# Preparing an attention stage inside the feed-forward before it, and another order of TensorE's work in each quad

## The reference

```
q = layernorm(x);  k = v = context                       # 16 blocks of 128 rows, causal in a block
scores = q @ k.T * 16**-0.5, masked;  p = exp(scores - max) / sum
x = x + tanh(g_xattn[1]) * (p @ v)
```

## Time and profile before

| | us |
|---|---|
| median of 3 runs | 1004.36 (1002.21 to 1005.16) |
| the profiled execution | 1005.2 |
| its span | 1003.1 |
| TensorE busy (PE) | 927.2, 92% of the span |
| VectorE busy (DVE) | 605.9, 60% |
| ScalarE busy (ACT) | 522.6, 52% |
| GpSimd busy (POOL) | 188.5, 19% |

### The profile page before, as it was taken

How to read it: one execution, slowest core, us unless ns; L and a number is a source line. 1 busy time by engine, 2 the same in 40 slices (tenths; PEclk the granted TensorE clock), 3 DMA queues, 4 the chain that set the end, 5 groups by cost and what they waited for, 6 DMA issues and landing times. The chain is left out here.

```text
span 1003.1 us, 14109 instructions
## 1 busy us (share of the span) xinstructions
PE 927.2 (92%) x4800; PEld 744.1 (74%) x4816; DVE 605.9 (60%) x1411; ACT 522.6 (52%) x938; POOL 188.5 (19%) x162
## 2 busy tenths in 40 slices
PE   6799889999999999778888886999999999999998
PEld 6799768877888888645555564787778888888886
DVE  6677654465645655367777754565865556555554
ACT  3222044433543333357677543666666676666665
POOL 5899200000000000166666400000000000000000
PEclk8899999999999999999999988999999999999999
DMA  9100110323211321225444213334444434544443
GB/s 309 35 1 1 64 64 17 110 86 110 69 49 48 106 80 47 95 81 157 150 143 131 94 64 100 127 126 126 140 144 128 140 106 137 147 143 141 145 128 116
DMA packets 58535, 105.43 MB, mean 105 GB/s; under 512 B 7360, under 2 KB 13888, under 8 KB 58080
## 3 DMA queue, kind: packets, MB, share of 16 engines
q1 hardware_dynamic: 57744, 104.39, 32.6%
q10 hardware_dynamic: 720, 0.14, 0.1%
HBM read 102.08 MB, written 2.42 MB: 104 GB/s over the span
## 5 line engine op out<-in xcount | busy, mean ns | idle before, releaser
L740 DVE TENSOR_TENSOR ylof<-yf,yhif 128x512 fp32r<-128x512 f32 x200 | 138.2, 691 | 176.2 <-ACT yhif L653 175.8
L884 PE MATMUL bank<-xhf,whif 128*128 128x512 f32 x528 | 212.2, 402 | 1.5 <-ACT rf L628 1.5
L884 PE MATMUL bank<-xlf,whif 128*128 128x512 f32 x528 | 208.7, 395 | 0.0
L884 PE MATMUL bank<-xhf,wlof 128*128 128x512 f32 x528 | 208.6, 395 | 0.0
L913 PE MATMUL bank<-yhif,whif 128*128 128x512 f32 x400 | 160.1, 400 | 13.0 <-DVE ylof L740 12.9
L653 ACT ACTIVATE yhif<-yf 128x512 fp32r<-128x512 f32 x200 | 125.5, 628 | 89.1 <-DVE yf L753 82.4
L913 PE MATMUL bank<-yhif,wlof 128*128 128x512 f32 x400 | 157.9, 395 | 0.0
L913 PE MATMUL bank<-ylof,whif 128*128 128x512 f32 x400 | 157.0, 393 | 0.0
L630 ACT ACTIVATE rf<-bank 128x512 f32<-128x512 f32 x136 | 81.6, 600 | 125.0 <-PE bank L884 124.2
L884 PEld LDWEIGHTS bank<-xhf,wlof 128*128 128x128 f32 x528 | 99.8, 189 | 24.0
L884 PEld LDWEIGHTS bank<-xhf,whif 128*128 128x128 f32 x528 | 99.4, 188 | 24.5 <-ACT rf L628 1.9
(11 more groups left out here) (129 smaller groups left out, 1197.2 us busy)
## 6 DMA issues: line engine op xcount, KB each, us to landing
Gf<-gates SPq DMA_DIRECT2D x160, 256.0 KB, 3.7
wrawf<-in_wu SPq DMA_DIRECT2D x68, 256.0 KB, 2.6
k_blocks_sb<-in_k_blk SPq DMA_DIRECT2D x64, 256.0 KB, 4.1
wrawf<-in_wu SPq DMA_DIRECT2D x32, 384.0 KB, 3.1
v_slot<-in_v_rows SPq DMA_DIRECT2D x16, 256.0 KB, 2.6
ctx_windows<-in_ctx_win SPq DMA_DIRECT2D x3, 1024.0 KB, 10.8
toeplitz<-in_kpad SPq DMA_DIRECT2D x4, 512.0 KB, 9.3
X<-in_x SPq DMA_DIRECT2D x4, 512.0 KB, 9.3
```

The lines of the kernel that those rows point to most:

```text
L740: dve.tensor_tensor(ylo[:, K % S, :], y[:, K % S, :], yhi[:, K % S, :].bitcast(F32), ALU.subtract).then_inc(s_yl, 1)
L884: last = pe.matmul(o, w_[:, Nu % S, wc], x_[:, c, xs], start=(m == 0), stop=(m == 5))
```

## The change

1. The attention's tiles and semaphores for keys, values and queries are set up ahead of f0, and its steps become functions that f0 can call: load_keys, key_hi, key_lo, query_normed, query_hi, query_lo, query_turned and query_copy (before: keys, k_hi, k_lo, normed, x_hi, x_lo, queries, q_copy).
2. In f0, SP issues six key loads, the mask, the bf16 identity and two value loads at step K = 48 (NK - 16). In the last twelve steps ScalarE and TensorE do three blocks' query_normed and query_hi, two blocks' query_turned and query_copy and four quads' key_hi; GpSimd does the low halves.
3. The last four pieces of f0's output are no longer turned and added in f0. Its tile (os_) outlives the stage, and the attention does this in its first quads: ffn_turned on TensorE and ffn_added on VectorE, interleaved with quads 0 to 3. variances("c", 1) and what follows from it move behind them.
4. The attention's keep_clock and first queries go. ScalarE's first instruction is an Exp on a small tile.
5. TensorE's order in iteration n becomes turned(n), scores(n+2), values(n). query_turned(b+2) comes in a block's last quad, a block earlier than before, and so do query_normed, query_hi and query_lo (b+3) on ScalarE and GpSimd. out_copy(b-1) and query_copy(b+1) are done in a block's first quad, the one ahead of and the other behind probs.

```diff
                     for j in range(BPB):
                         residual(NB - BPB + j)
 
+
+        pn = ExitStack()
...
+        def load_keys(sp, n):
+            if n >= KLR:
+                sp.wait_ge(s_k2, n - KLR + 1)
+            sp.dma_start(KM[:, n % KLR, :], k_blk[n]).then_inc(s_kl[n % KLR], 16)
+
+        def load_values(sp, b):
+            if b >= 2:
+                sp.wait_ge(s_pv, 4 * (b - 2) + 4)
+            sp.dma_start(V[:, b % 2].rearrange("p h d -> p (h d)"), v_rows[b]).then_inc(s_vl[b % 2], 16)
...
+        def key_hi(act, n):
+            act.wait_ge(s_kl[n % KLR], LOADED + 16 * (n // KLR + 1))
+            if n >= KR:
+                act.wait_ge(s_s, n - KR + 1)
+            act.activation(K1[:, n % KR, :], KM[:, n % KLR, :], ACT.Copy).then_inc(s_k1, 1)
...
+        def key_lo(pool, n):
+            pool.wait_ge(s_k1, n + 1)
+            pool.tensor_tensor(K2[:, n % KR, :], KM[:, n % KLR, :], K1[:, n % KR, :].bitcast(F32),
+                               ALU.subtract).then_inc(s_k2, 1)
...
+        def query_normed(act, b):
+            act.wait_ge(s_sh, b // (2 * BPB) + 1)
+            if b >= 2:
+                act.wait_ge(s_lo, b - 1)
+            act.activation(xc[:, b % 2, :], X[:, b, :], ACT.Identity, bias=nshift[:, b:b + 1],
+                           scale=rstd[:, b:b + 1]).then_inc(s_n, 1)
...
+        def query_lo(pool, b):
+            pool.wait_ge(s_hi, b + 1)
+            pool.tensor_tensor(xs[:, b % 2, :, 1, :], xc[:, b % 2, :].rearrange("p (q f) -> p q f", q=4),
+                               xs[:, b % 2, :, 0, :].bitcast(F32), ALU.subtract).then_inc(s_lo, 1)
+
+        def query_turned(pe, b):
+            pe.wait_ge(s_lo, b + 1)
+            if b > 0:
+                pe.wait_ge(s_qt, b)
+            for t in range(4):
+                last = pe.transpose(x_bank[:, t * P:(t + 1) * P],
+                                    xs[:, b % 2, t].rearrange("p s f -> p (s f)").bitcast(F32), ident[:])
+            last.then_inc(s_xt, 1)
...
+        def query_copy(act, b):
+            act.wait_ge(s_xt, b + 1)
+            if b >= 2:
+                act.wait_ge(s_s, 4 * (b - 1))
+            act.activation(Q1[:, b % 2].rearrange("p t q -> p (t q)"), x_bank, ACT.Copy, scale=SCALE1).then_inc(s_qt, 1)
...
+        def attention_loads(sp):
+            for n in range(KLR):
+                load_keys(sp, n)
+            sp.dma_start(causal[:], causal_c).then_inc(s_cc, 16)
+            sp.dma_start(identb[:], identb_c).then_inc(s_cc, 16)
+            load_values(sp, 0)
+            load_values(sp, 1)
+
+        def attention_ahead_act(act, left):
+
+            if left in (12, 11, 4):
+                query_normed(act, {12: 0, 11: 1, 4: 2}[left])
+            if left in (11, 10, 3):
+                query_hi(act, {11: 0, 10: 1, 3: 2}[left])
+            if left in (9, 8, 7, 6):
+                key_hi(act, 9 - left)
+            if left in (6, 3):
+                query_copy(act, {6: 0, 3: 1}[left])
+
+        def attention_ahead_pe(pe, left):
+
+            if left in (8, 5):
+                query_turned(pe, {8: 0, 5: 1}[left])
+
+        def attention_ahead_pool(pool):
+            query_lo(pool, 0)
+            query_lo(pool, 1)
+            for n in range(KR):
+                key_lo(pool, n)
+            query_lo(pool, 2)
...
+                def out_turned(pe, p, s, i, dst):
+                    pe.wait_ge(s_os, 2 * p + s + 1)
+                    for j in (2 * i, 2 * i + 1):
+                        for c in range(2):
+                            last = pe.transpose(dst[:, (j % 2) * D + c * P:(j % 2) * D + (c + 1) * P],
+                                                os_[:, s, c, j * P:(j + 1) * P], ident[:])
+                    last.then_inc(s_ot, 1)
+
+                def out_added(dve, p, s, i, src):
+                    n = 4 * p + 2 * s + i
+                    dve.wait_ge(s_ot, n + 1)
+                    b0 = n * 2
+                    xv = X[:, b0:b0 + 2, :].rearrange("p b d -> p (b d)")
+                    dve.tensor_tensor(xv, src, xv, ALU.add).then_inc(s_xa, 1)
+                    if not final:
+                        dve.wait_ge(s_xa, n + 1)
+                        for b in (b0, b0 + 1):
+                            dve.bn_stats(stats[:, b, :], X[:, b, :]).then_inc(s_xs, 1)
+
...
@@ -598,6 +733,8 @@
                                 if GATES_STORE[m] == K:
                                     store_gates(m)
                             gate_rows(K)
+                            if not final and K == NK - 16:
+                                attention_loads(sp)
...
                         if not final:
                             deviations(pool, "c", 0)
                             shifts(pool, "c", 0)
+                            attention_ahead_pool(pool)
...
+                            if not final:
+                                attention_ahead_act(act, NK - K)
                         if not gated:
...
@@ -867,9 +999,10 @@
                                 negated(dve, "c", 0)
                         if not gated:
                             y_lo(NK - 1)
-                        for s in range(2):
-                            for i in range(2):
-                                residual(1, s, i, bk(2 * s + i))
+                        if final:
+                            for s in range(2):
+                                for i in range(2):
+                                    residual(1, s, i, bk(2 * s + i))
...
-                        pe.wait_ge(s_xa, 4)
-                        for s in range(2):
-                            for i in range(2):
-                                out_t(1, s, i, bk(2 * s + i))
+                            if not final:
+                                attention_ahead_pe(pe, NK - K)
+                        if final:
+                            pe.wait_ge(s_xa, 4)
+                            for s in range(2):
+                                for i in range(2):
+                                    out_t(1, s, i, bk(2 * s + i))
+
+            return out_turned, out_added, s_xa, s_xs
...
 
             def turn_bank(n):
                 return bk(4 + n % 2)
@@ -1172,70 +1280,27 @@
             with nc.Block() as block:
                 @block.sync
...
-                    vals(1)
                     for n in range(KLR, NQ):
-                        keys(n)
-                        if n % 4 == 0 and n // 4 + 1 < NB and n // 4 >= 2:
-                            vals(n // 4)
-                    vals(NB - 1)
+                        load_keys(sp, n)
+                        if n % 4 == 0 and n // 4 >= 2:
+                            load_values(sp, n // 4)
 
                 @block.gpsimd
...
                     for n in range(NQ):
                         b, t = n // 4, n % 4
                         if n + KR < NQ:
-                            k_lo(n + KR)
-                        if t == 3 and b + 2 < NB:
-                            x_lo(b + 2)
+                            key_lo(pool, n + KR)
+                        if t == 3 and b + 3 < NB:
+                            query_lo(pool, b + 3)
+                        if n == 4:
+                            deviations(pool, "c", 1)
+                            shifts(pool, "c", 1)
                         if n == 4 * 10:
                             deviations(pool, "f1", 0)
 
...
-                    keep_clock(pe, bk(0), 20)
-                    queries(0)
                     pe.wait_ge(s_cc, 32)
                     scores(0)
                     scores(1)
+                    ffn_turned(pe, 1, 0, 0, o_bank)
+                    ffn_turned(pe, 1, 0, 1, row_bank)
                     for n in range(NQ):
                         b, t = n // 4, n % 4
+                        turned(n)
                         if n + 2 < NQ:
                             scores(n + 2)
-                        turned(n)
-                        if n > 0:
-                            values(n - 1)
-                        if t == 0 and b + 1 < NB:
-                            queries(b + 1)
+                        if n == 0:
+                            pe.wait_ge(s_ffn_x, 5)
+                        values(n)
+                        if n in (1, 2):
+                            pe.wait_ge(s_ffn_x, 5 + n)
+                            ffn_turned(pe, 1, 1, n - 1, row_bank)
+                        if t == 3 and b + 2 < NB:
+                            query_turned(pe, b + 2)
+                        if n == 6:
+                            pe.wait_ge(s_ffn_x, 8)
                         if t == 2 and b > 0:
                             out_rows(b - 1)
-                    values(NQ - 1)
                     out_rows(NB - 1)
...
-                    normed(0)
-                    x_hi(0)
-                    k_hi(0)
-                    normed(1)
-                    k_hi(1)
-                    q_copy(0)
-                    x_hi(1)
-                    k_hi(2)
-                    k_hi(3)
```

(87 more changed lines are left out.)

91 lines of the change are left out of this document (9 added, 82 removed).

## The result

The changed kernel takes 974.59 us (median of 4 runs, 973.37 to 975.51) against 1004.02 (4 runs) for the kernel before on the same chip: a ratio of 0.9708 with a 95% interval of [0.9689, 0.9726]. The forecast was 975. The profiled execution took 974.85, with a span of 972.7 in place of 1003.1.

A forecast was written before the change was run, and what follows sets the result against it. The attention's stride was taken as bound by the order in which engines wait for each other, none full. Start 14.9 plus stride 15.4 less tail 0.8 made 29.5 off 1005.2, 975.7, stated as 975; range 967 to 986.

The forecast's parts named there:

- f0's end: In f0's last steps, two added query_turned cost 0.9 us; the other work put there is hidden.
- Start: Where f0 ends and the attention begins: turned(6) comes at 431.1 instead of 446.01, 14.9 us less.
- the ten short instructions: On VectorE in the attention's start, variances and negated between shifted(4) and maxima(5): an estimated 0.8 us.
- Stride: Attention's 14 blocks, turned(6) to turned(62): 7.7 us a block, 108.2 in all against 123.6, 15.4 less.
- a new wait: In each attention quad, values wait 0.18 us for probs of the same quad: 1.35 from turned against TensorE's 1.17.
- TensorE's own: In each attention quad, TensorE's own order from turned is done at 1.17 us, before the values can start.
- two late keys: In the stride, first keys landing after 3.9 us in 2 blocks make the cycle 8.1, adding 2 x 0.4.
- Tail: From turned(62) to f1's start: 7.4 us instead of 6.6, a loss of 0.8.
- Key loads as the bound: Rival in the stride: first keys land after 3.9 as a rule, 8.2 us a block, 981.9 us; chance 0.17.
- The new order bringing nothing: Rival in the stride: a block stays at 8.83 us, only start and tail change, 991.1 us; chance 0.08.
- Half clock: Rival in the attention: TensorE at half clock, a block of about 11 us, 1021 us; chance 0.05.
- the rule weighed: Skill's rule on TensorE's clock: short idle spells repeated each iteration swing it between two levels, against values waiting every quad.

The follow-up runs named there:

- e9: Changed kernel with values(n-1) in place of values(n) behind turned(n) and scores(n+2), and a third values slot: 968.16 us, ratio 0.9648.
- e6: Changed kernel with a third slot for the values: 973.86 us, ratio 0.9702.
- e10: The kernel of e6 (changed kernel, third values slot) run once more beside e9: 973.00 us, ratio 0.9689.
- e11: e9 with two values slots and load_values(b) issued behind keys(4b+5) instead of ahead of keys(4b+1): 967.74 us, ratio 0.9646.
- e12: e9 with two values slots and the values' load where the changed kernel has it, ahead of keys(4b+1): 987.14 us, ratio 0.9827.
- e8: Changed kernel with load_values(b) waiting one quad more, for values(4b-4) instead of values(4b-5): 998.87 us, ratio 0.9952.
- e4: Kernel before with the new TensorE order and queries two blocks ahead, nothing prepared in f0: 988.38 us, ratio 0.9839.
- e1: Changed kernel with TensorE's order put back to scores(n+2), turned(n), values(n-1): 990.39 us, ratio 0.9861.

## Why the prediction was right

**f0's end.** Predicted 0.9 more. ScalarE's Silu marks f0's steps in the changed kernel:

```profile
377.20 0.60 ACT L766 ACTIVATE rf<-bank 128x512 f32<-128x512 f32 x1 [0.84 <-PE bank L1017]
381.38 0.60 ACT L766 ACTIVATE rf<-bank 128x512 f32<-128x512 f32 x1 [0.84 <-PE bank L1017]
386.02 0.60 ACT L766 ACTIVATE rf<-bank 128x512 f32<-128x512 f32 x1 [1.30 <-PE bank L1017]
390.20 0.60 ACT L766 ACTIVATE rf<-bank 128x512 f32<-128x512 f32 x1 [0.36 <-PE bank L1017]
394.38 0.60 ACT L766 ACTIVATE rf<-bank 128x512 f32<-128x512 f32 x1 [1.36 <-PE bank L1017]
399.01 0.60 ACT L766 ACTIVATE rf<-bank 128x512 f32<-128x512 f32 x1 [1.33 <-PE bank L1017]
```

A step is 4.18; the two with a query_turned in them are 4.64 and 4.63, so 0.91 for both. SP issues its ten loads at 330.6 to 336.1. The step there, which has one of the first half's out_t in it, is 4.64 against 4.62 in the kernel before, and those in which ScalarE does the new copies are 4.18. These were hidden, as said.

**Start.** The chain on VectorE was right to the hundredth for a quad (2.70). turned(6) came at 431.75 in place of 431.1, since turned(5) came at 430.05, 0.65 later than in the sum. The term that was too small is the ten short instructions: they put maxima(5) off by 1.31 (427.27 to 428.58) where 0.8 was estimated, and maxima(0) was 0.14 late already. The gain is 14.3 where 14.9 stood.

**Stride.** A quad of 1.70 (1.71), a block of 7.68 (7.7). Within the quad, the 0.18 called a new wait was too large: e9, which has none, needs 1.62, so it is 0.08, and the rest is TensorE's own: 1.26 where 1.17 stood, a figure read from a stretch that ends in turned and not in the values, whose weight load comes later; the sum did not depend on it. turned(62) is at 539.22, so 14 blocks take 107.5 (108.2). The gain is 123.6 - 107.5 = 16.1 where 15.4 stood.

One term of it had the wrong cause. The 0.8 set aside for two late keys did not occur: with a third slot nothing changes (e6, e10), and in the changed kernel the first key behind the values landed after 2.8 to 3.1 in all 14 blocks that have one. One block of 8.0 is there, but it is GpSimd's:

```profile
501.06 1.64 POOL L137 TENSOR_TENSOR rstd<-vpe,mhalf 128x8 f32<-128x8 f32 x1
502.67 3.95 POOL L505 TENSOR_TENSOR k_blocks_lo<-k_blocks_sb,k_blocks_hi 128x512 fp32r<-128x512 f32 x3
504.00 0.19 PEld L1312 LDWEIGHTS bank<-k_blocks_hi,q_split_t 128*128 128x128 f32 x1 [0.54 <-POOL k_blocks_lo L505]
```

deviations("f1", 0) comes once, at n = 40, ahead of a key's low half. e9 and e11, in which ScalarE waits for no key, have a block of 8.0 at the same place. The prediction saw GpSimd's queue for the query and not for this. With it 14 x 7.68 - 0.4 + 0.33 is the 107.5 measured.

**Tail.** 7.34 from turned(62) to f1, with 7.4 predicted and 6.6 before:

```profile
539.22 0.66 PE L1320 MATMUL bank<-ident,shifted_scores 128*128 128x128 f32 x4
543.85 0.66 PE L1340 MATMUL bank<-ident,o_t 128*128 128x128 f32 x4 [0.72 <-ACT o_t L1379]
546.56 1.19 PE L110 MATMUL bank<-ident 128*128 128x128 f32 x4 [2.06 <-PEq L1280]
```

Sum: 14.3 + 16.1 - 0.75 = 29.65, which is 576.21 - 546.56. The span shrank by 30.4; the other 0.75 lies in f1, which the change does not touch and which took 424.0 to 427.1 in the fourteen profiles.

That the total came so close is partly luck. The start was 0.6 short of its term and the stride 0.7 above its own, and f1 gave 0.75 that no term stood for. The mechanism is not luck: each part was found at its size by itself.

**The rivals.** Key loads as the bound: not in the changed kernel, but they lie 0.5 a block away. One quad's lateness of the values, by their order or by the wait, costs 13 to 26 us (e12, e8). The prediction gave this case 0.17, but by another cause, keys that land late in a tighter burst, and that did not occur. For so narrow a slack it was not too much. The new order bringing nothing: refuted by e4. Half clock: refuted, 1.00 in the stride. With it the rule weighed falls for this kernel. The Trainium skill, "TensorE: Matmul & The Clock Gate", section "A second HAM failure mode: psum-queue depth-cycling", tells of a kernel of bf16 matmuls, 512 columns wide, in which short idle spells between groups of matmuls make the clock swing; here the weight load of the values stands idle for 0.44 in each of 56 quads, and the clock stays at 1.00 in the stride.

## What to carry to other kernels

Where engines take turns, the order within one iteration is a quantity of its own: exchanging turned and scores, with the same work and the same slots, was worth 12.8 us of 142, and 5.4 where a late load held the kernel up. Look in each in-order list for an instruction that waits with something urgent behind it: in e11, moving the one values' load behind the key loads did what a further buffer did. And before an order is judged slow, take such a wait away first, since e1 hid a merely slower order behind late loads.

## What the runs showed that was not expected

VectorE's add to x (residual), with both tensors in on-chip memory and none in a bank, has no fixed price. Its durations (minimum, median, maximum in ns), first in the changed kernel:

```profile
L1422 DVE SCALAR_TENSOR_TENSOR X<-o_norm,tg,X x14: 483/485/1069, 435.3 to 535.5; 128x256 f32<-128x256 f32 x14
```

and in e1_prepared_old_order:

```profile
L1424 DVE SCALAR_TENSOR_TENSOR X<-o_norm,tg,X x12: 484/869/1405, 435.5 to 536.9; 128x256 f32<-128x256 f32 x12
```

The long ones go with a subtraction on GpSimd: the one of 1.07 in the changed kernel, at 504.41, lies within GpSimd's 3.95 above, and the short ones there lie in its pauses but for at most 0.2. In e1 the nine that are not 0.48 (0.59 to 1.41) each end 0.27 to 0.29 after a subtraction has ended, as if they had waited for it. The maxima and shifted, which read a bank, stay at 0.63 to 0.69 beside the same subtractions. So an order may shorten an instruction on another engine; that the subtraction is the cause was not tested by a run, and how much of the gain this is was not tried apart.

The 2.6 us by which f0's first step moves between executions (its first Silu at 133.4 to 133.8 in eight profiles, 135.9 to 137.1 in the other six) arise in the stage before f0. What decides them stays open. They are over half of the 4.3 that part e11 from the changed kernel, so a single execution's span does not rank the two.
